# Who sends the row of maxima: ACT's own DMA queue in place of SP's, in a transformer block with cross attention and an expert FFN

## The chip, the cores and the metric

The kernel runs on one core of one Trainium2 chip. The metric is the device time of one execution in microseconds (us), lower is better; the time of before is a median of three executions. The engines are TensorE (PE), VectorE (DVE), ScalarE (ACT), GpSimd (POOL) and SyncE (SP); each runs its own list of instructions in order and waits on semaphores for the others. Before the change SP issues every plain DMA of the kernel, POOL the indirect ones, ACT none.

## The reference

For 8 batches of 512 tokens and width 256:

```
x = x + cross_attention(layernorm(x), ctx, ctx, w_proj, b_proj)   # 16 heads of 16
x = x + expert_ffn(layernorm(x), Wg, W1, W2, W3)                  # 8 experts, top 2, hidden 682
```

The attention's scores are softmax(q k / 4) over 512 keys for each of 16 heads. The kernel subtracts each query's maximum before the exponential, and that maximum is what the change is about.

## The kernel before, in words

**Attention (slots).** The first half of the execution is an order written out by hand in slots: `for slot in range(FIRST, LAST)` stands in each engine's list, and every step has a slot at which it is due, counted from its batch's first one. A batch takes 16 slots (`PER = H`); two halves of a slot do one unit each, so a batch has 32 units of scores of each of two kinds:

- `scores_ts` (line 1155): queries on the partitions. DVE takes the maximum of each row with a minus sign into `neg_max` (line 902).
- `scores_st` (line 1168), eight slots later (`AT_EXP = 8`): keys on the partitions. Here the maximum of a query runs along the free axis, so it can't be a bias. It goes in as one more row of the contraction: partition `64 * par + STACK` of `q_stack` holds the negative maximum, against a row of ones in `k_stack` (hence 49 rows, and not 48). ACT takes the exponential into `probs` (line 785), and PE weighs the values with it (line 1183).

Both kinds use the same three PSUM pairs of banks in turn. PE can fill a pair only when ACT (exponential) or DVE (maximum) has read what stood in it.

**The row of maxima.** For each batch there are four groups `g` of four heads. When DVE has the maxima of a group, PE turns them (four transposes into the miscellaneous bank, line 1197), ACT copies the 4 x 512 row to `max_row[g % 2]` in SBUF (line 802), and two DMAs of 2 KB each (`par` 0 and 1) carry it to partitions 48 and 112 of `q_stack`. `scores_st` waits for `s_mrow[g]` before the first unit of the group. The copies stand at half slots 8, 18, 26 and 34 of a batch, that is in slots 4, 9, 13 and 17; the groups' first exponentials stand in slots 8, 12, 16 and 20.

**SP's list.** SP waits for ACT's copy in slots 4, 8, 12 and 16 (`AT_MAX_ROW + 4 * g`) and then issues the two DMAs (line 567). The same list has the loads of `x_in`, `kt_in`, `v_ext`, `x_res`, the six DMAs of `k_stack` (line 549, slot 10 for the next batch) and six of `q_stack` (line 557), the stores of the FFN's split weights (line 477, after POOL's `w_lo`, slots 1, 6 and 14) with the next load of `w_in` behind them (line 468), and, in slot 17 of the last batch, `load_first_tiles` (line 503 and on), the first loads of the FFN. What stands behind a wait of SP waits too. The k parts are held by `s_kl` and by `s_b`, the scores of the batch before the current one, whose last unit is in slot 7; the copy into `k16[0]` that overwrites their source (ACT, line 864, slot 12) waits for them to land.

**ACT's list.** In each slot: exponential of half 0, miscellaneous copies of half 0 (`misc(2 * slot)`), exponential of half 1, then the copy of `heads`, the weights' upper halves (line 774), normalisations (line 790), casts, and the miscellaneous copies of half 1. All four copies of maxima stand in a half 0.

**FFN (tiles).** From about 510 us on the tokens of each expert go through two matmul layers, tile by tile; nothing of the change is in that part.

Of the kernel before, what the change touches and what calls it, by code (L numbers as in the profile page):

```python
# [18 lines left out]
STACK = 3 * D  # L19
# [74 lines left out]
AT_MAX_ROW = 4  # L94
# [45 lines left out]
def due(step, offset, of=1):  # L140

    b, left = divmod(step - offset, PER * of)
    return [b] if left == 0 and 0 <= b < B else []


def running(slot, offset):

    b, s = divmod(slot - offset, PER)
    return [(b, s)] if 0 <= b < B else []
# [8 lines left out]
def misc_use(b, name, i):  # L158
    return MISC_USE[b, name, i]


def misc_at(half_slot):
    return [MISC_AT[half_slot]] if half_slot in MISC_AT else []
# [86 lines left out]
def build(nc, xq_l, x_l, v_l, kT_l, wp_l, bias, wg_l, w12_l, w3_l, const, out):  # L250
    ctx = ExitStack()
    with ctx:
# [41 lines left out]
        max_row = [sa(f"max_row{i}", [4, T], F16) for i in range(2)]  # L294
# [62 lines left out]
        q_stack, k_stack, v_ext, probs = (q_stack0, q_stack1), (k_stack0, k_stack1), (v_ext0, v_ext1), (probs0, probs1)  # L357
# [98 lines left out]
        def _(sp):  # L456
# [76 lines left out]
            for slot in range(FIRST, LAST):  # L533
                for b in due(slot, AT_X_IN):
                    if b >= 1:
                        sp.wait_ge(s_ql, b)
                        sp.dma_start(x_in[:, :, :], xq_l[b]).then_inc(s_xin, 16)
                for b in due(slot, AT_K_IN):
                    if b >= 1:
                        sp.wait_ge(s_kl, b)  # L540
                        sp.dma_start(kt_in[:, :, :], kT_l[b]).then_inc(s_kin, 16)
                for b in due(slot, AT_K_PARTS):
                    sp.wait_ge(s_kl, b + 1)
                    if b >= 2:
                        sp.wait_ge(s_b, (b - 1) * UNITS)
                    for j, part in enumerate((0, 1, 0)):
                        for par in range(2):
                            row = 64 * par + j * D
                            sp.dma_start(k_stack[b % 2][row:row + D, :, :], k16[part][:, par, :]).then_inc(s_kd, 16)
                for b in due(slot, AT_Q_PARTS):  # L550
                    sp.wait_ge(s_mr, misc_use(b, "turn_q", 1) + 1)
                    if b >= 2:
                        sp.wait_ge(s_b, (b - 1) * UNITS)
                    for j, part in enumerate((0, 0, 1)):
                        for par in range(2):
                            row = 64 * par + j * D
                            sp.dma_start(q_stack[b % 2][row:row + D, :, :], qt16[part][:, par, :]).then_inc(s_qd, 16)
                for b in due(slot, AT_V_IN):
                    if b >= 2:
                        sp.wait_ge(s_pv, (b - 1) * 4)  # L560
                    sp.dma_start(v_ext[b % 2][:, :, :, :], v_l[b]).then_inc(s_vin, 16)
                for g in range(4):
                    for b in due(slot, AT_MAX_ROW + 4 * g):
                        sp.wait_ge(s_mr, misc_use(b, "max", g) + 1)
                        for par in range(2):
                            row = 64 * par + STACK
                            sp.dma_start(q_stack[b % 2][row:row + 1, 2 * g:2 * g + 2, :],
                                         max_row[g % 2][2 * par:2 * par + 2, :]).then_inc(s_mrow[g], 16)
                for c, off in enumerate(AT_W_OUT):
                    for e in due(slot, off):  # L570
                        keep_weights(e, c)
                for b in due(slot, AT_X_RES):
                    if b >= 1:
                        sp.wait_ge(s_mr, misc_use(b - 1, "project", 3) + 1)
                    sp.dma_start(x_res[:, :, :], x_l[b]).then_inc(s_xres_ld, 16)
                for b in due(slot, AT_X2_OUT):
                    sp.wait_ge(s_mr, misc_use(b, "project", 3) + 1)
                    hold(sp, s_held[3])
                    if b >= 1:
                        sp.wait_ge(s_x2st, b * 16)  # L580
                    sp.dma_start(out_v[b], x2[:, :, :]).then_inc(s_x2st, 16)
                if slot == 0:
                    sp.wait_ge(s_cst, 5)
                    sp.dma_start(out[TOKENS:TOKENS + SLOTS, :].rearrange("(s p) c -> p s c", p=P),
                                 fill[:, :, 0:W]).then_inc(s_pad, 16)
                    sp.dma_start(z_dram[E * REGION:E * REGION + SLOTS, :].rearrange("(s p) c -> p s c", p=P),
                                 fill[:, :, :]).then_inc(s_pad, 16)
                for h in range(2):
                    if piece_at(2 * slot + h):
                        next(early)  # L590
                for b in due(slot, AT_EARLY_LOAD):
                    if b == B - 1:
                        load_first_tiles()
# [171 lines left out]
        def _(act):  # L765
# [11 lines left out]
            def exponentials(slot, half):  # L777
                for b, s in running(slot, AT_EXP):
                    g, a, k = s // 4, s // 2, 2 * (s % 2) + half
                    u = b * UNITS + 2 * s + half  # L780
                    act.wait_ge(s_b, u + 1)
                    if s % 4 == 0 and half == 0 and b * 4 + g >= 2:
                        act.wait_ge(s_pv, b * 4 + (g - 1))
                    j = 2 * (a % 2)
                    nc.scalar.activation(probs[g % 2][:, j:j + 2, k, :], pair_banks[PLACE["exp", u] % 3], ACT.Exp,  # L785
                                         scale=0.25).then_inc(s_exp, 1)
# [6 lines left out]
            def misc(half_slot):  # L793
                for m, name, i, b in misc_at(half_slot):
# [10 lines left out]
                    if name == "turn_q":  # L805
                        ge(act, s_qd, b * 96)
                        nc.scalar.copy(qt16[i][:, :, :].rearrange("p a t -> p (a t)"), misc16).then_inc(s_mr, 1)

            def keep_turned(k, par):
                act.wait_ge(f_turn, k + 1)  # L810
                nc.scalar.copy(zt16[par][:, :, :, :].rearrange("p k a s -> p (k a s)"), turn16).then_inc(f_zt, 1)  # L811
# [31 lines left out]

            for slot in range(FIRST, LAST):
                exponentials(slot, 0)
                misc(2 * slot)
                if piece_at(2 * slot):
                    next(early)
                exponentials(slot, 1)
                for b, s in running(slot, AT_WEIGH):  # L850
                    if s % 4 == 3:
                        g = s // 4
                        q = b * 4 + g
                        act.wait_ge(s_pv, q + 1)
                        if q >= 2:
                            act.wait_ge(s_mw, misc_use((q - 2) // 4, "heads", (q - 2) % 4) + 1)
                        nc.scalar.copy(heads[q % 2][:, :], pv_bank).then_inc(s_hd, 1)  # L857
                for c, off in enumerate(AT_W_HI):
                    for e in due(slot, off):
                        high_weights(e, c)  # L860
                for b in due(slot, AT_K_HI):
                    act.wait_ge(s_kin, (b + 1) * 16)
                    ge(act, s_kd, b * 96)
                    nc.scalar.copy(k16[0][:, :, :], kt_in[:, :, :]).then_inc(s_kh, 1)
                for i in range(NT):
                    for b in due(slot, AT_X_NORM[i]):
                        act.wait_ge(s_rstd, (b + 1) * 4)
                        normalise(x_in, x_in, rstd, shift, i, s_qn)
                    for b in due(slot, AT_Z_NORM[i]):
                        act.wait_ge(s_rstd2, (b + 1) * 4)  # L870
                        ge(act, s_zl, b)
                        normalise(z_n, x2, rstd2, shift2, i, s_zn)
                for b in due(slot, AT_Q_HI):
                    act.wait_ge(s_qn, (b + 1) * NT)
                    if b >= 1:
                        act.wait_ge(s_mw, misc_use(b - 1, "turn_q", 1) + 1)
                    nc.scalar.copy(q16[0][:, :, :], x_in[:, :, :]).then_inc(s_qh, 1)
                for b in due(slot, AT_Z_HI):
                    act.wait_ge(s_zn, (b + 1) * NT)
                    ge(act, s_sc, b * 128)  # L880
                    nc.scalar.copy(z_row[:, 0, :, 0:W // 2].bitcast(F16), z_n[:, :, :]).then_inc(s_zh, 1)
                misc(2 * slot + 1)
                if piece_at(2 * slot + 1):
                    next(early)
# [481 lines left out]
```

## Time and profile before

| what | us |
|---|---|
| median of three executions | 984.34 |
| lowest and highest | 981.7, 991.81 |
| the profiled execution, own time | 979.42 |
| its span in the profile | 977.5 |
| attention, from the span's start | 0 to about 510 |
| FFN | about 510 to 977.5 |

The profiled execution is one more execution, not one of the three. Its own time is 1.9 us over its span; it lies 4.9 us below the median of the three. TensorE's mean granted clock was 0.963 of full speed.

### The profile page before, as it was taken

What the parts mean: (1) busy time and instruction counts of PE and PEld (TensorE: products, weight loads), DVE (VectorE), ACT (ScalarE), POOL (GpSimd) and SP (SyncE); (2) the same over time, 40 slices, a digit from 0 to 9 for tenths busy, and PEclk for the clock granted to TensorE, in tenths of its full rate; (3) what the DMA queues carried; (4) which work ended last, traced back from release to release, by engine and by line L of the source; (5) the groups of instructions that cost most, each with busy time, mean ns of one, the idle gap of its engine ahead of it and who ended that gap; (6) DMA issues with size and microseconds to landing.
All of it is one profiled execution on the core that took longest, in us unless ns stands there. A gap on an engine that the chain in (4) does not pass through costs nothing. (4 is left out here: it accounts for less than half of the span.)

```text
span 977.5 us, 20608 instructions
## 1 busy us (share of the span) xinstructions
PE 839.7 (86%) x6800; PEld 521.4 (53%) x6800; DVE 592.1 (61%) x1215; ACT 592.3 (61%) x951; POOL 447.6 (46%) x408
## 2 busy tenths in 40 slices
PE   0478898979789888899878987699999999999995
PEld 0112233323233322333236866599898998898995
DVE  1587887867778687797714554245445554545553
ACT  3368898987888778778683524244444444444442
POOL 4444456766858667685523644122332222233222
PEclk9998999999999999999899989799999999999998
DMA  6774746758476675555172649577543645254641
GB/s 168 191 151 157 179 153 191 146 194 169 155 195 137 219 159 180 120 145 186 60 264 83 216 131 297 161 226 225 154 130 97 178 131 138 43 163 120 198 80 22
DMA packets 66475, 154.28 MB, mean 158 GB/s; under 512 B 7280, under 2 KB 45296, under 8 KB 62576
## 3 DMA queue, kind: packets, MB, share of 16 engines
q1 hardware_dynamic: 52976, 135.63, 47.7%
q0 software_dynamic: 13440, 17.90, 9.4%
q8 instruction: 33, 0.54, 0.2%
q14 instruction: 26, 0.21, 0.1%
HBM read 129.43 MB, written 42.55 MB: 176 GB/s over the span
## 5 line engine op out<-in xcount | busy, mean ns | idle before, releaser
L902 DVE TENSOR_REDUCE neg_max<-ps 128x2 f16<-128x1024 f32 x256 | 307.7, 1220 | 80.0 <-PE ps L1155 78.6
L785 ACT ACTIVATE probs<-ps 128x1024 f32<-128x1024 f32 x256 | 257.5, 1022 | 66.1 <-PE ps L1168 64.2
L699 POOL DMA_INDIRECT out<-y,aim x72 | 112.9, 1568 | 289.1 <-DVE y L1100 240.1
L1270 PE MATMUL ps<-zt,w 128*128 128x256 f16 x792 | 217.1, 274 | 1.1 <-ACT zt L811 1.1
L1272 PE MATMUL ps<-zt,w 128*128 128x256 f16 x792 | 217.1, 274 | 0.0
L1274 PE MATMUL ps<-zt,w 128*128 128x256 f16 x792 | 217.0, 274 | 0.0
L823 ACT ACTIVATE silu<-ps 128x256 f32<-128x256 f32 x216 | 82.4, 382 | 203.2 <-PE ps L1274 196.3
L1082 DVE SCALAR_TENSOR_TENSOR hid<-ps,silu 128x256 f32<-128x256 f32 x216 | 91.7, 425 | 137.0 <-ACT silu L823 133.6
L1155 PE MATMUL ps<-k_stack,q_stack 48*128 48x512 f16 x512 | 106.9, 417 | 58.1 <-ACT probs L785 36.5
L1183 PE MATMUL ps<-probs,v_ext 128*32 128x512 f32 x1024 | 145.4, 641 | 6.1 <-ACT heads L857 5.1
L686 POOL TENSOR_TENSOR w_in<-w_in,scale_w 128x1408 f32<-128x1408 f32 (+1 forms) x24 | 62.6, 2607 | 130.6 <-ACT w_hi L774 130.5
L1168 PE MATMUL ps<-q_stack,k_stack 49*128 49x512 f16 x512 | 104.8, 407 | 10.8 <-DVE neg_max L902 9.4
L1290 PE MATMUL ps<-w,hid 128*128 128x256 f16 x360 | 100.5, 279 | 4.4 <-DVE hid L1089 4.4
L1292 PE MATMUL ps<-w,hid 128*128 128x256 f16 x360 | 100.5, 279 | 0.0
L1294 PE MATMUL ps<-w,hid 128*128 128x256 f16 x360 | 100.3, 279 | 0.0
L1270 PEld LDWEIGHTS ps<-zt,w 128*128 128x128 f16 x792 | 78.0, 98 | 12.3 <-ACT zt L811 1.3
L1168 PEld LDWEIGHTS ps<-q_stack,k_stack 49*128 49x128 f16 x512 | 25.3, 95 | 110.7 <-issue 59.4
L1100 DVE TENSOR_SCALAR y<-ps,aim 128x256 f32<-128x256 f32 x72 | 31.5, 480 | 86.4 <-PE ps L1299 86.4
L1272 PEld LDWEIGHTS ps<-zt,w 128*128 128x128 f16 x792 | 77.9, 98 | 9.7
L1274 PEld LDWEIGHTS ps<-zt,w 128*128 128x128 f16 x792 | 77.9, 98 | 9.4
L1155 PEld LDWEIGHTS ps<-k_stack,q_stack 48*128 48x128 f16 x512 | 25.4, 96 | 105.0 <-ACT probs L785 74.0
L1089 DVE TENSOR_TENSOR hid<-hid 128x256 f16<-128x256 f32 x180 | 77.7, 432 | 1.3 <-ACT hid L831 0.2
(122 smaller groups left out, 1124.4 us busy)
## 6 DMA issues: line engine op xcount, KB each, us to landing
w<-w_parts SPq DMA_DIRECT2D x36, 1408.0 KB
w<-w_parts SPq DMA_DIRECT2D x36, 768.0 KB
w_in<-in_w SPq DMA_DIRECT2D x16, 704.0 KB, 5.4
z_in<-slots SPq DMA_DIRECT2D x37, 258.0 KB, 5.3
v_ext<-in_v SPq DMA_DIRECT2D x8, 1024.0 KB, 7.7
k_stack<-k SPq DMA_DIRECT2D x48, 128.0 KB, 4.7
q_stack<-qt SPq DMA_DIRECT2D x48, 128.0 KB, 6.9
w_in<-in_w SPq DMA_DIRECT2D x8, 768.0 KB, 5.2
```

The lines of the kernel that those rows point to most:

```text
L699: nc.gpsimd.indirect_dma_start(out=out, out_offset=bass.IndirectOffsetOnAxis(ap=aim[frm][:, t, 0:1].bitcast(U32), axis=0), in_=y[frm][:, t ...
L785: nc.scalar.activation(probs[g % 2][:, j:j + 2, k, :], pair_banks[PLACE["exp", u] % 3], ACT.Exp, scale=0.25).then_inc(s_exp, 1)
L902: nc.vector.tensor_reduce(neg_max[b % 2][:, i, c:c + 3:2], pair_banks[PLACE["max", u] % 3], AX.X, ALU.max, negate=True).then_inc(s_red, 1)
L1155: mm = nc.tensor.matmul(to[:, par, :], q_stack[r][rows, a, i * P:(i + 1) * P], k_stack[r][rows, a, :], start=True, stop=True)
L1168: mm = nc.tensor.matmul(to[:, par, :], k_stack[r][rows, a, k * P:(k + 1) * P], q_stack[r][rows, a, :], start=True, stop=True)
L1183: mm = nc.tensor.matmul(pv_bank[32 * n:32 * n + 32, :], v_ext[b % 2][:, j, 4 * g + n, :], probs[g % 2][:, n, j, :], start=(j == 0), stop=( ...
L1270: nc.tensor.matmul(dst, w[:, kk, 1, cols], z16[:, kk, 0, :], start=(kk == 0), stop=False)
L1272: nc.tensor.matmul(dst, w[:, kk, 0, cols], z16[:, kk, 1, :], start=False, stop=False)
L1274: mm = nc.tensor.matmul(dst, w[:, kk, 0, cols], z16[:, kk, 0, :], start=False, stop=(kk == 1))
L1290: nc.tensor.matmul(y_bank[t], h[1], w3[par][:, 0, m, :], start=first, stop=False, skip_group_check=True)
L1292: nc.tensor.matmul(y_bank[t], h[0], w3[par][:, 1, m, :], start=False, stop=False, skip_group_check=True)
L1294: nc.tensor.matmul(y_bank[t], h[0], w3[par][:, 0, m, :], start=False, stop=False, skip_group_check=True)
```

## The change

SP's four waits a batch and its 64 DMA issues are taken out. ACT gets a function `send_rows`, called in each half slot right behind the exponential: if a copy of maxima stood in the half slot before, it waits for its own copy (`s_mr`), and issues the same two DMAs on ACT's queue. Since all copies stand in half 0, the rows are sent in half 1, behind that half's exponential and ahead of the other steps of the half.

```
@@ SP
-                for g in range(4):
-                    for b in due(slot, AT_MAX_ROW + 4 * g):
-                        sp.wait_ge(s_mr, misc_use(b, "max", g) + 1)
-                        for par in range(2):
-                            row = 64 * par + STACK
-                            sp.dma_start(q_stack[b % 2][row:row + 1, 2 * g:2 * g + 2, :],
-                                         max_row[g % 2][2 * par:2 * par + 2, :]).then_inc(s_mrow[g], 16)
@@ ACT
+            def send_rows(half_slot):
+                for m, name, g, b in misc_at(half_slot - 1):
+                    if name == "max":
+                        act.wait_ge(s_mr, m + 1)
+                        for par in range(2):
+                            row = 64 * par + STACK
+                            nc.scalar.dma_start(q_stack[b % 2][row:row + 1, 2 * g:2 * g + 2, :],
+                                                max_row[g % 2][2 * par:2 * par + 2, :]).then_inc(s_mrow[g], 16)
@@ ACT, the loop over slots
                 exponentials(slot, 0)
+                send_rows(2 * slot)
                 misc(2 * slot)
                 if piece_at(2 * slot):
                     next(early)
                 exponentials(slot, 1)
+                send_rows(2 * slot + 1)
```

## Rows read from the trace of the kernel before

**Rows 1.** The page: span, and busy time, share and instructions of each engine.

```profile
span 977.5 us, 20608 instructions
PE 839.7 (86%) x6800; PEld 521.4 (53%) x6800; DVE 592.1 (61%) x1215; ACT 592.3 (61%) x951; POOL 447.6 (46%) x408
```

**Rows 2.** Busy time by stretch: start:end, length, each engine, granted clock, DMA share, GB/s.

```profile
60.00:120.00 60.00, 48.85 (x328) 12.68 (x326) 46.13 (x53) 49.24 (x57) 26.13 (x14) 0.94 0.67 160
...
420.00:480.00 60.00, 51.36 (x359) 17.72 (x361) 50.25 (x94) 45.10 (x54) 35.95 (x38) 0.96 0.39 137
...
510.00:977.00 467.00, 433.48 (x4005) 382.55 (x4004) 221.56 (x614) 201.56 (x480) 145.54 (x125) 0.96 0.53 149
```

**Rows 3.** Waits, 60 to 480 us: who for whom, us in total, times, longest.

```profile
DVE neg_max L902 <- PE ps L1155: 63.9, 89, 2.7
...
ACT probs L785 <- PE ps L1168: 52.9, 66, 3.9
...
PE ps L1155 <- ACT probs L785: 36.2, 55, 2.2
...
ACT k L864 <- DMA k_stack<-k: 3.0, 3, 1.7
...
PE ps L1168 <- DMA q_stack<-max_row: 0.7, 1, 0.7
```

**Rows 4.** Waits of SP's queue, 60 to 480 us.

```profile
SPq L567 <- ACT max_row L802: 141.0, 24, 12.0
SPq L477 <- POOL w_lo L689: 128.4, 19, 12.8
```

**Rows 5.** The row's DMA issues: count, ns min/median/max, first and last start.

```profile
L567 SPq DMA_DIRECT2D q_stack<-max_row x64: 558/565/730, 44.2 to 490.0; - x64
```

**Rows 6.** Timeline of SP, one batch: start us, us, engine, line, out<-in, count.

```profile
221.20 0.46 SPq L468 DMA_DIRECT2D w_in<-in_w  x1
226.05 1.17 SPq L567 DMA_DIRECT2D q_stack<-max_row  x2
227.32 3.87 SPq L549 DMA_DIRECT2D k_stack<-k  x6
231.29 3.81 SPq L557 DMA_DIRECT2D q_stack<-qt  x6
...
252.47 1.18 SPq L567 DMA_DIRECT2D q_stack<-max_row  x2
```

**Rows 7.** Timeline of ACT around copies of maxima with dense work behind.

```profile
251.88 0.56 ACT L802 COPY max_row<-ps 4x512 f16<-4x512 f16 x1
252.35 1.01 ACT L785 ACTIVATE probs<-ps 128x1024 f32<-128x1024 f32 x1
253.26 0.58 ACT L790 ACTIVATE x_in<-x_in,shift,rstd 128x256 f32<-128x256 f32 x1
253.88 1.04 ACT L877 CAST q<-x_in 128x1024 f16<-128x1024 f32 x1
```

**Rows 8.** Timeline of ACT and SP around the last copy of maxima.

```profile
489.32 1.01 ACT L785 ACTIVATE probs<-ps 128x1024 f32<-128x1024 f32 x1
489.44 1.17 SPq L567 DMA_DIRECT2D q_stack<-max_row  x2
...
490.96 1.02 ACT L785 ACTIVATE probs<-ps 128x1024 f32<-128x1024 f32 x1 [0.63 <-PE ps L1168]
...
494.11 1.64 SPq L503 DMA_DIRECT2D z_in<-slots  x2
```

**Rows 9.** Timeline around the one time that PE waited for a row.

```profile
109.40 0.47 SPq L468 DMA_DIRECT2D w_in<-in_w  x1
...
110.14 1.17 SPq L567 DMA_DIRECT2D q_stack<-max_row  x2
...
116.54 0.39 PE L1168 MATMUL ps<-q_stack,k_stack 49*128 49x512 f16 x2 [0.70 <-DMA q_stack<-max_row]
```

**Rows 10.** Waits of SP's queue, 470 to 620 us.

```profile
SPq L516 <- DMA slots<-z_row,slot_u: 2.2, 1, 2.2
```

**Rows 11.** Timeline of SP: a load's issue that took longer.

```profile
125.44 1.39 SPq L468 DMA_DIRECT2D w_in<-in_w  x1
```

## The prediction, made before the changed kernel ran

> **What bounds the kernel now.** I read four views in this order. The page's first part [rows 1] gives PE 86% of the span and no other engine over 61%, but that is a mean over two halves with different limits. The table by stretches [rows 2] parts them: in the FFN, from 510 us on, PE is busy 433.5 of 467 us and ACT only 201.6; in the attention PE, DVE and ACT are all busy some 75 to 90% of each 60 us. The change touches only the attention, so at most some 450 us of the span are open to it. The waits [rows 3] say how the three engines hold each other there: DVE waits 63.9 us for PE, ACT 52.9 us for PE, and PE 36.2 us for ACT's exponentials, since all use three pairs of banks in turn. PE is busy 360.4 of the 420 us from 60 to 480 (the seven stretches of that table, the first and the last of which stand in [rows 2]; the five between them are 53.82, 51.12, 51.77, 51.10 and 52.36), so it idles 59.6 us, and 36.2 of these, 0.61, end with an exponential. With the small waits for ACT's other copies I take 0.65 as the share of an extra microsecond on ACT that comes through to the end. That is an estimate; the ends are 0.3 (ACT itself is idle about a fifth of the stretch, so a delay can be caught up) and 1.
>
> Then SP. It waits 141.0 us for ACT's copies of maxima and 128.4 us for POOL's `w_lo` [rows 4]. This looks like a prize and is not one: SP computes nothing, and its waiting costs only what somebody else then waits for. Those who wait for its transfers in the steady part are ACT before the copy into `k16`, 3.0 us in 3 times, and PE before `scores_st`, 0.7 us once [rows 3].
>
> **Removed from SP.** 64 issues of 565 ns [rows 5], 36 us of SP's time, and four waits a batch. What moves: in the batch shown, SP is done with a load at 221.66, then stands until the second group's row at 226.05, and only then issues the six k parts at 227.32 and the six q parts until 235.1 [rows 6]. The k parts' own conditions (POOL's `w_lo` of the slot, scores of slot 7) are met at about 221.7, so they start some 5.6 us earlier. ACT's 3.0 us of waiting for them disappear: 3.0 x 0.65 = 2.0 us gained. The other steps behind SP's row waits are stores of weights that wait for POOL anyway, and loads with slots to spare, costed at nothing; their cover is that no engine is recorded as waiting for them in the steady part. `load_first_tiles` gains nothing: its row's issue ended at 490.6, yet it started at 494.1 [rows 8], because it then waited 2.2 us for the scatter of tokens [rows 10], and that stays.
>
> **The row itself.** In 27 of 32 cases SP already stood waiting and issued within 0.03 us of the copy's end: the copy of [rows 7] ends at 252.44, SP issues at 252.47 [rows 6]. So the rows don't leave earlier. In ACT's queue they are no longer lined up behind SP's bulk transfers. PE waited for a row once, when it was issued 0.74 us after a 704 KB load: 0.70 us [rows 9]. Gain 0.7 us, if the own queue gets them through sooner; zero otherwise. The landing then took up to 5.2 us from the end of the issue (111.3 to 116.5); a row is wanted three slots, some 11 us, after its copy, so even beside the k and q parts, which will now be in flight at the second group's row, I expect no new wait.
>
> **Added to ACT.** 32 times: a wait for its own copy, and two issues. No ACT issue is in the trace; the nearest rows are SP's for the same transfers, 1.17 us for two [rows 6, 8]. Queued behind them on ACT are, in half 1 of the slot, the normalisations, casts, copies of `heads` and weights, and the next exponential, for which PE waits. Lower bound: SP's issues of larger transfers take 0.46 us in [rows 6], two such are 0.92 us, a little less than the exponential in front. Upper bound below. I take 1.17, as it is the same transfer.
>
> How much shows: the exponential in front is already handed to the engine, which can compute while ACT's sequencer issues. In [rows 7] the copy ends at 252.44, the exponential runs 252.35 to 253.36 and the next instruction started at 253.26. Issues from 252.47 hold the sequencer to 253.64: a delay of 0.38 us. I went through all 32 copies so: 25 have the next instruction right behind the exponential (delays of 0.31 to 0.44 us by this reckoning, 0.38 the value of the example), and 7 have a gap behind it that swallows the issue, such as the last, where the next exponential came only at 490.96 [rows 8]. Sum: 25 x 0.38 = 9.5 us of ACT.
>
> **Two queues at once.** The k and q parts, 3.87 + 3.81 us for 12 issues or 0.64 us each [rows 6], will start at about 221.7 and run to 229.5, and ACT issues the second group's row at 226.05: in the middle, in 7 of 8 batches. No row of before shows two plain queues issuing together. Bounds: nothing, or a whole issue of SP's for each of ACT's two, 1.28 us x 7 = 9.0 us. I take half, 4.5 us (an arrival at random waits half an issue), since issues of SP's do stretch at times, 1.39 us for one of 0.46 [rows 11, 6]. The Trainium skill has a rule that speaks against the change here ("Perfetto Trace Analysis", DMA Instruction — HWDGE): the block that makes descriptors is shared by the two engines that issue such DMAs, it is locked for one of them, and the lock wait is inside the issue that the profile shows. By it the term would be between 4.5 and 9.0 us and not nothing; no row here can show it. Its "DMA: Bandwidth & Descriptors" (Issuing engines are not separate DMA queues) adds that spreading DMAs over engines saves only issue time.
>
> **The sum.** ACT: 9.5 + 4.5 = 14.0 us more, 3.0 us less waiting: 11.0 x 0.65 = 7.2 us. PE's wait for a row: -0.7. Together +6.5 us, of which I take 6: 979.4 + 6 = 985.4 us for an execution like the profiled one. That one is 4.9 us below the median of the three; on the median I get 984.3 + 6 = 990.3. Since four executions of before (with the profiled one) have a middle of 983, I write 989.
>
> **Rivals.**
> - *Hidden issue.* If ACT's issues are as short as SP's short ones (0.92 us for two), the exponential hides them, and with no contention what is left is the gain: -2.0 - 0.7 = -2.7 us, 981.6 on the median. For: many issues of SP's are that short. Against: this very transfer took 558 ns at the least [rows 5].
> - *No overlap.* ACT issues only when the exponential has ended, or stalls its engine. Then each of 25 costs 1.17 + 0.09 (the overlap of neighbours in [rows 7]) = 1.26 us: 31.5 + 4.5 - 3.0 = 33.0 x 0.65 - 0.7 = +20.8 us, 1005 us. Place: the instruction behind each row's send. It decides once the delay behind a send is over 0.7 us: 25 x 0.7 + 4.5 - 3.0 = 19.0 x 0.65 is over 1%. Against: the trace's ACT instructions overlap by 0.09 us, so the sequencer runs ahead. For: ACT has not issued a DMA before, so nothing shows how the two share the sequencer.
> - *Contention and full pass-through.* The upper end of the two queues (9.0), and 0.1 us more at each send to get the emptied engine going (the cast of [rows 7], which waits for its own engine's result, starts 0.04 us behind the end, where others start 0.09 us before it, 0.13 us lost): 9.5 + 3.3 + 9.0 - 3.0 = 18.8 x 0.8 - 0.7 = +14.3, about 998 us.
> - *Faster by over 1%.* It would need some 10 us, and all recorded waits for SP's transfers in the steady part come to 3.7. It takes a wait whose recorded cause is another engine. I can't find it in the rows.
>
> **Chances.** My forecast (between +2 and +9.8 us) 0.50; hidden issue or otherwise about nothing or a small gain 0.18; contention with high pass-through 0.12; no overlap 0.13; faster by over 1% 0.07. One per cent, 9.8 us, is about what a measurement of this kernel tells from no change: its three executions span 10.1 us. So faster 0.07, same 0.68, slower 0.25. The range reaches from a gain of 6 us, 978 us, to the no-overlap case's centre less a little, 1004 us; that leaves out about 0.06 below and half of no overlap, and a little of contention, above. The forecast's own range is 985 to 994.
>
> **What would show it.** In the profile after: rows of ACT's queue with the two issues, about 0.57 us each, more where SP issues k and q parts at the same time; the instruction behind them 0.3 to 0.45 us later than the exponential's end in place of 0.09 us before it; k parts right behind the load of slot 6, 5 us earlier against the copy of maxima; no wait of ACT for `k_stack` in the steady part; PE's waits for ACT's exponentials up by some 6 us; the FFN's length unchanged. Wrong if the issues of ACT are much shorter or longer than SP's, if the exponential in front does not run beside them, if PE begins to wait for rows, or if SP, now ahead, starts bulk transfers that collide with something that I costed at nothing.

## The result and the profile after

Over 20 executions of each, the changed kernel takes 995.02 us (median; 988.22 to 1006.65), before 984.11 us (976.5 to 992.57). The ratio is 1.0117, with a 95% interval of 1.0095 to 1.0139: slower by 1.2%, some 11.5 us. The ratio and its interval leave out the runs that lie over 1.5% above the fastest of their kernel. Forecast were 989 us and about no change. The profiled execution has a span of 987.3 us, 9.8 us more than before's 977.5 [rows 1].

The page's first part, as [rows 1]; the work is the same, the span is not:

```profile
span 987.3 us, 20608 instructions
PE 842.6 (85%) x6800; PEld 521.6 (53%) x6800; DVE 593.0 (60%) x1215; ACT 595.0 (60%) x951; POOL 448.1 (45%) x408
```

The waits between engines from 60 to 480 us, as [rows 3] (line numbers have moved: 1155 is 1160, 1168 is 1173, 785 is 778, 902 is 907, 864 is 869):

```profile
DVE neg_max L907 <- PE ps L1160: 69.4, 101, 2.7
...
ACT probs L778 <- PE ps L1173: 47.6, 61, 2.1
...
PE ps L1160 <- ACT probs L778: 33.4, 55, 2.2
PE ps L1173 <- DMA q_stack<-max_row: 14.0, 7, 3.0
...
ACT probs L778 <- issue: 2.7, 8, 0.4
...
ACT o_t L797 <- issue: 2.2, 7, 0.3
ACT x_in L783 <- issue: 2.0, 6, 0.4
...
ACT k L869 <- DMA k_stack<-k: 1.0, 1, 1.0
```

Three things are to be seen. PE's waits for ACT's exponentials did not go up, as forecast, but down, from 36.2 to 33.4 us. PE's wait for the row of maxima went from 0.7 us, once, to 14.0 us in 7 times: once in each of the first seven batches, at the second group. And ACT has a new kind of idle time, "issue", in pieces of 0.3 to 0.4 us: the exponential, the `o_t` copy and the `x_in` row hold 6.9 us of it.

The waits of SP's queue in the same stretch, as [rows 4]: the 141.0 us for ACT's copies are gone, and the wait for POOL's `w_lo` is 174.9 us longer.

```profile
SPq L477 <- POOL w_lo L682: 303.3, 22, 22.7
SPq L541 <- POOL k L718: 9.9, 5, 4.1
```

The timeline of the same batch, one engine after the other, as [rows 6]; ACTq is ACT's own queue:

```profile
222.77 0.46 SPq L468 DMA_DIRECT2D w_in<-in_w  x1
223.33 4.09 SPq L549 DMA_DIRECT2D k_stack<-k  x6
227.52 5.13 SPq L557 DMA_DIRECT2D q_stack<-qt  x6
```

```profile
225.69 0.57 ACT L795 COPY max_row<-ps 4x512 f16<-4x512 f16 x1 [0.28 <-PE ps L1202]
226.17 1.01 ACT L778 ACTIVATE probs<-ps 128x1024 f32<-128x1024 f32 x1
226.29 1.21 ACTq L809 DMA_DIRECT2D q_stack<-max_row  x2
227.55 1.02 ACT L778 ACTIVATE probs<-ps 128x1024 f32<-128x1024 f32 x1 [0.37 <-issue]
...
233.79 0.39 PE L1173 MATMUL ps<-q_stack,k_stack 49*128 49x512 f16 x2 [1.80 <-DMA q_stack<-max_row]
```

The k parts now start at 223.33, 2.93 us before the copy ends at 226.26; in [rows 6] they started at 227.32, behind the row. The row leaves ACT between 226.29 and 227.50, beside them, and PE gets it only at 233.79, 6.3 us later. PE had been ready at 231.99. Over the seven batches the k parts start 0.1 to 4.3 us before the copy ends, and PE gets the row 5.9 to 7.5 us after its issues. The k parts themselves land later too: the median from issue to landing is 6.8 us, before 4.7.

How long ACT's issues took, as [rows 5]:

```profile
L809 ACTq DMA_DIRECT2D q_stack<-max_row x64: 565/566/1201, 44.1 to 496.1; - x64
```

The attention ends 6.1 us later in this pair of profiles: the last `scores_st` starts at 509.7 us, before at 503.6. The rest of the 9.8 us comes in the first tiles of the FFN, at the two loads of tokens that PE waits for before and after (PE starts behind them at 621.68 and 641.50, before at 614.70 and 631.67). PE's two waits there are 16.3 us together, before 13.9. I made no run on that part.

### The profile page after: what moved, and what is told of

It is laid out like the page before. It is cut to its first block and busy times, and to the rows that moved or that the text cites. A ratio compares the mean times of both kernels' runs of the same rounds, so it can differ in the third digit from the quotient of the medians.

```text
span 987.3 us, 20608 instructions
## 1 busy us (share of the span) xinstructions
PE 842.6 (85%) x6800; PEld 521.6 (53%) x6800; DVE 593.0 (60%) x1215; ACT 595.0 (60%) x951; POOL 448.1 (45%) x408
```

## The experiments

All edits are against the changed kernel or the kernel before, as said; each ratio is to the kernel before on the same chip, with its 95% interval. Two theories stand against each other. *Collision*: SP, freed of its wait for the second group's copy, sends the k and q parts ahead of and beside that group's row, and the row lands too late. *Stall*: the issues hold ACT's sequencer, and what shows behind the exponential is the loss.

**SP keeps its waits, ACT sends.** Changed kernel, with the waits back in SP's list and no row to send behind them:

```
+                for g in range(4):
+                    for b in due(slot, AT_MAX_ROW + 4 * g):
+                        sp.wait_ge(s_mr, misc_use(b, "max", g) + 1)
```

> ACT sends all rows as in the changed kernel, but SP keeps its four waits a batch for the copies of maxima, so that its k and q parts start when they did before. Collision theory (the loss is PE's wait for the second group's row, which now travels beside the 12 k and q parts): if what matters is that the parts start no earlier, PE's waits for rows fall from 14.0 to under 3 us and the ratio to before to about 1.003; if a row on a queue of its own loses to the parts even when both start together, PE still waits 5 to 14 us and the ratio stays near 1.01. Stall theory (the loss is ACT's sequencer, 25 delays of some 0.35 us): PE's waits for rows may go, yet the ratio stays at about 1.010.

Ratio 1.0023 [0.9998, 1.0049]. Its waits from 60 to 480 us have no wait of a PE matmul for a row, and ACT's idle time from issues is what it was in the changed kernel:

```profile
ACT probs L781 <- issue: 3.0, 8, 0.4
...
ACT x_in L786 <- issue: 2.0, 6, 0.4
ACT o_t L800 <- issue: 2.0, 6, 0.4
```

So with all 32 sends on ACT the kernel is 0 to 5 us slower than before, and giving SP nothing but its old waits takes away most of the loss. It was mostly the timing of SP's other transfers that mattered, not who sends the row.

**Second group's row on SP, the others on ACT.** ACT's `send_rows` for g in (0, 2, 3), SP's old code for g = 1.

> The second group's row stays on SP, ahead of the k and q parts as before; ACT sends the other three (24 of 32 sends). Collision theory: PE's waits for rows are under 1 us, the ratio is 1.000 to 1.004. Stall theory: three quarters of the delays are left, the ratio is about 1.009.

Ratio 1.0066 [1.0041, 1.0092], between the two. PE doesn't wait for rows, as the collision theory has it, but the ratio is above its 1.004 and below the stall theory's 1.009. It was run again, below.

**Only the second group's row on ACT.** The reverse: ACT sends 8 of 32 rows, SP the rest, so SP no longer waits for the second group's copy.

> Only the second group's row is sent by ACT (8 of 32 sends), the others by SP as before. Collision theory: PE waits for this row about 14 us in 7 times as in the changed kernel, the ratio is 1.008 to 1.012. Stall theory: a quarter of the delays, the ratio is about 1.003.

Ratio 1.0118 [1.0070, 1.0166], the whole loss with a quarter of the sends. Its waits from 60 to 480 us:

```profile
PE ps L1180 <- DMA q_stack<-max_row: 17.4, 7, 3.6
```

Here the stall theory, as the cause of most of the loss, fell.

**All rows on SP, the second group's behind the parts.** Kernel before, one number:

```
-                    for b in due(slot, AT_MAX_ROW + 4 * g):
+                    for b in due(slot, 10 if g == 1 else AT_MAX_ROW + 4 * g):
```

> ACT sends nothing. SP sends all rows, but the second group's only after the k and q parts of slot 10, so that the parts start early and the row stands behind them in the one queue. Collision theory: the row leaves about 3 us later than from ACT and then lines up behind 1.5 MB, PE waits 14 to 35 us for it, the ratio is 1.01 to 1.03. Stall theory: no delay of ACT, the ratio is 1.000.

Ratio 1.0515 [1.0475, 1.0555]: the direction was right, the size far over what was expected. No ACT issue at all, and the suspected cost enlarged:

```profile
PE ps L1168 <- DMA q_stack<-max_row: 47.4, 7, 9.9
```

47.4 us of PE waiting cost some 50 us of time, about one for one.

**Waits kept, and ACT's two issues parted.** As the first, but `send_rows` issues `par` 0 one half slot behind the copy and `par` 1 two half slots behind it, so each stands behind its own exponential:

```
+                for par in range(2):
+                    for m, name, g, b in misc_at(half_slot - 1 - par):
+                        if name == "max":
```

> As the run with SP's waits kept, but ACT issues one DMA of 0.57 us behind each of two exponentials in place of two behind one. If the 0.35 us delays behind the sends are what is left of the loss (1.0023), they vanish from ACT's idle time (8.1 us recorded as issue, to under 1) and the ratio is 0.998 to 1.001. If ACT's delays are absorbed anyway, the ratio stays at 1.002.

Ratio 0.9990 [0.9962, 1.0018]. Around a copy with dense work behind it, to be set beside [rows 7]:

```profile
193.99 0.56 ACT L798 COPY max_row<-ps 4x512 f16<-4x512 f16 x1
194.45 1.01 ACT L781 ACTIVATE probs<-ps 128x1024 f32<-128x1024 f32 x1
194.57 0.57 ACTq L812 DMA_DIRECT2D q_stack<-max_row  x1
195.37 0.58 ACT L786 ACTIVATE x_in<-x_in,shift,rstd 128x256 f32<-128x256 f32 x1
195.98 1.05 ACT L885 CAST q<-x_in 128x1024 f16<-128x1024 f32 x1
196.10 0.57 ACTq L812 DMA_DIRECT2D q_stack<-max_row  x1
```

The instruction behind the exponential starts 0.92 us after it, as in before (0.91): one issue of 0.57 us fits under an exponential of 1.01 us, two don't. No wait of ACT for an issue is left in the stretch; PE waits 1.9 us, in 2 times, for rows. Against the first run this is 0.0033, but with an interval of about 0.004 either way it is not clear of nothing. It is the best of the versions with ACT as sender, and the same as before within its interval.

**Only the wait for the second group's copy kept.** As the first, with `for g in (1,)`.

> ACT sends all rows; SP keeps only the wait for the second group's copy, the one ahead of the k and q parts. If this single wait is what was lost, the ratio is that of the run with all four waits, 1.002, within 0.003. If SP's freedom elsewhere costs too (the run with the second group's row on SP had 1.0066 without any wait for rows, and its PE clock rose some 20 us later at the start), it is about 1.006.

Ratio 1.0024 [1.0000, 1.0048]. One wait of SP's four does what the four did, within the intervals.

**Parts held until the row has landed.** Changed kernel, and ahead of the k parts:

```
+                    if b >= 1:
+                        sp.wait_ge(s_mrow[1], b * 32)
```

> The changed kernel with the k parts held until both DMAs of the second group's row have landed: the row travels with no parts beside it. Collision theory: no wait of PE for rows; the parts start 2 to 4 us after the copy and land later, so that ACT waits up to 3 us a batch before its copy into k16. Ratio 1.003 to 1.010, made of ACT's waits and not PE's. Stall theory: the changed kernel's 1.012.

Ratio 1.0104 [1.0060, 1.0147]: just over the range that was expected. PE doesn't wait for rows; ACT waits instead, for the late k parts ahead of its copy into `k16` (from 60 to 480 us):

```profile
ACT k L871 <- DMA k_stack<-k: 9.7, 6, 3.3
```

So early parts and late parts both cost here, by different waits. This run also measures how fast a row lands with no parts beside it, since SP's next issue is what it lets go. The timeline of ACT's and SP's queues:

```profile
175.31 1.19 ACTq L811 DMA_DIRECT2D q_stack<-max_row  x2
177.59 1.87 SPq L551 DMA_DIRECT2D k_stack<-k  x3
236.78 1.17 ACTq L811 DMA_DIRECT2D q_stack<-max_row  x2
239.03 1.20 SPq L551 DMA_DIRECT2D k_stack<-k  x2
```

From the end of the row's issues (176.50, 237.95) to SP's first k part it takes 1.1 us, as in five of the seven batches, against 5.9 to 7.5 us in the changed kernel. In the other two a load of SP's left shortly ahead of the row: 2.3 us, and 3.4 us in the second batch, where 768 KB started 0.75 us before it.

**Only the q parts held.** Changed kernel; SP waits for the second group's copy between the k and the q parts.

> The changed kernel with only the six q parts held behind the second group's copy; the six k parts leave early as in the changed kernel, ahead of the row. If it is the transfers in front of the row that hold it, most of the wait stays (8 to 14 us of PE in 7 times, ratio 1.008 to 1.012). If it is what comes in beside and behind it, most goes (under 5 us, ratio 1.002 to 1.005).

Ratio 1.0084 [1.0053, 1.0114]; PE waits as long as ever:

```profile
PE ps L1175 <- DMA q_stack<-max_row: 16.9, 7, 3.4
```

But the edit held almost nothing. In the changed kernel the q parts start only when the k parts' six issues are done, 0.05 to 0.10 us behind them; here they start 0.10 to 0.32 us behind them:

```profile
224.27 4.07 SPq L549 DMA_DIRECT2D k_stack<-k  x6
228.64 4.77 SPq L559 DMA_DIRECT2D q_stack<-qt  x6
228.65 1.31 ACTq L811 DMA_DIRECT2D q_stack<-max_row  x2
236.26 0.39 PE L1175 MATMUL ps<-q_stack,k_stack 49*128 49x512 f16 x2 [1.93 <-DMA q_stack<-max_row]
```

So this run doesn't part the k parts from what comes behind the row. It is nearly a repeat of the changed kernel, and shows that two nearly equal kernels can come out 0.0033 apart, 1.0084 and 1.0117, which is within their intervals. The second batch, with a load of 768 KB 0.7 us ahead of the row in all four cases, tells more of the order. From the end of the row's issues to landing it took 3.4 us with no parts in flight (the run before), 5.2 with the k parts right behind the row ([rows 9]), at most 5.2 with both started together (the first run), and 5.9 with the k parts 0.17 us ahead of it (the changed kernel). By these four, one profile each, what comes right behind the row slows it too, and what goes ahead slows it a little more, past the slack.

**The same order, with the row in SP's queue.** Kernel before; SP issues the k parts, waits for the copy, issues the row, then the q parts.

> ACT sends nothing. SP issues the six k parts early, then waits for the second group's copy and issues its row, then the six q parts: the timing of the run with the q parts held, with the row in SP's queue and not in ACT's. If a queue of its own brings the row past transfers that were issued earlier, PE waits longer here than the 16.9 us of that run, 20 us or more, and the ratio is 1.012 or more. If the queue makes no difference, PE waits 14 to 19 us, and the ratio is 1.005 to 1.010 (no delays of ACT).

PE waits 16.7 us in 7 times, in total the same as the 16.9 with the row in ACT's queue:

```profile
PE ps L1175 <- DMA q_stack<-max_row: 16.7, 7, 5.5
```

The equal totals are chance, though. In the first two batches the copy was ready while SP was still issuing k parts, so the row left 2.4 and 4.3 us behind the copy, and PE waited 4.6 and 5.5 us (with ACT as sender 2.5 and 1.9). In the other five the row left at most 1.2 us behind the copy, and PE waited 6.6 us together, against 12.5. One batch of each kind:

```profile
109.71 4.39 SPq L549 DMA_DIRECT2D k_stack<-k  x6
114.15 1.29 SPq L555 DMA_DIRECT2D q_stack<-max_row  x2
121.01 0.61 PE L1175 MATMUL ps<-q_stack,k_stack 49*128 49x512 f16 x2 [5.46 <-DMA q_stack<-max_row]
...
233.16 1.30 SPq L555 DMA_DIRECT2D q_stack<-max_row  x2
234.56 4.34 SPq L564 DMA_DIRECT2D q_stack<-qt  x6
239.61 0.39 PE L1175 MATMUL ps<-q_stack,k_stack 49*128 49x512 f16 x2 [0.67 <-DMA q_stack<-max_row]
```

From the end of its issues the row took 4.9 to 6.3 us here, ahead of the q parts, and 6.1 to 7.8 us in ACT's queue with the q parts starting beside it. So the k parts ahead of the row are enough for a wait, and ACT's queue did not bring the row past them; it took about 1 us longer there, and whether the q parts beside it or the queue make that, the runs don't part. The ratio is 1.0151 [1.0114, 1.0187], above the expected 1.010, and what is in it beside the row's wait stays open. TensorE's mean granted clock over the timed runs was 0.949 here and 0.955 in the run with the q parts held, so part of it may come with the clock; that is not shown.

**Second group's row on SP, again.**

> The kernel with the second group's row on SP and the others on ACT once more, on another chip. Its 1.0066 stood above the 1.0023 and 1.0024 of two kernels with more sends on ACT. If that was scatter (its profile had a late rise of PE's clock), it comes out at 1.000 to 1.004 now; if it is the kernel, at 1.005 to 1.008.

Ratio 1.0065 [1.0030, 1.0100]: not scatter. Part of it shows in the pace of PE in the first batch. The `scores_ts` matmuls take 610 to 620 ns at first and 384 later. In both profiles of this kernel the step comes at some 85 to 91 us, in the changed kernel's at about 70. The granted clock reads 1.00 in all of these stretches, so it is the length of the matmuls that shows the step. In the kernel before, from 72 to 78 us, they take 614 to 623 ns at a granted clock of 0.50: the slow pace is that of the lower level, 1.2 GHz. Here is the kernel's second profile from 70 to 80 us, then the changed kernel's (count, busy us, mean ns):

```profile
L1167 PE MATMUL ps<-k_stack,q_stack 48*128 48x512 f16 x8 | 2.5, 611 | 1.7 <-ACT probs L785 1.7
```

```profile
L1160 PE MATMUL ps<-k_stack,q_stack 48*128 48x512 f16 x14 | 2.7, 383 | 2.6 <-ACT probs L778 2.6
```

But the profile of the run that keeps only the second group's wait has the late step too, at 1.0024. Why this kernel is slower than that one is open.

**The changed kernel with ACT's two issues parted.** SP without waits, `send_rows` as in the fifth run.

> The changed kernel with ACT's two issues parted, one behind each of two exponentials; SP free of waits as in the changed kernel. The collision stays and the second DMA of the row leaves up to 1.5 us later: PE's waits for rows 14 to 22 us. ACT's delays go. Collision theory: the ratio stays at 1.009 to 1.014. Stall theory: 1.000 to 1.004.

Ratio 1.0080 [1.0051, 1.0110]; PE waits 15.1 us for rows, ACT none for issues. Less than the 1.009 expected, and 0.0037 less than the changed kernel, as between the first and the fifth run (0.0033). But the run that nearly repeats the changed kernel has 1.0084, about the same.

## Why the prediction was wrong

What the runs give, in parts of the time before: the collision, 0.0094 (1.0117 - 1.0023) or 0.0090 (1.0080 - 0.9990), each give or take 0.003 to 0.004; with the near repeat in the changed kernel's place, 0.0061. ACT's delays, 0.0033 and 0.0037 (the two pairs with and without parted issues), each with about as much uncertainty, and 0.0004 with the near repeat. So more than half of the 1.0117 is the collision, 6 to 9 us, and ACT's delays are somewhere from nothing to some 4 us. That the two terms add up to about the whole is no test, since all four are differences of the same four ratios; what speaks for them is that each comes out alike both ways. The kernel with the second group's row on SP, 0.0042 slower than the one with SP's waits kept and with fewer sends on ACT, fits neither term and is open. The forecast had ACT's term and not the collision.

- **The step that failed** is the one on the row itself: "even beside the k and q parts, which will now be in flight at the second group's row, I expect no new wait", priced at -0.7 us. It came to 6 to 9 us more, with 14.0 us of PE's waiting. Both of its numbers were off. The slack was put at "three slots, some 11 us", from a mean slot; at the second group it is 5.7 us (copy's end 226.26, PE ready 231.99). [Rows 9] held the same: the row's issues from 110.14, PE ready at 115.84. And the landing was taken from that same case, 5.2 us behind one load (of 768 KB, not 704: ACT's next `w_hi` has 1536 columns), as an upper bound; behind six k parts it is 5.9 to 7.5 us, alone 1.1 us. Read together there, the slack from the start of the row's issues is 5.7 us, and 1.2 us of issues with 5.2 of landing are 6.4. That is 0.7 us too much, the wait recorded there, and no room at all.
- **"SP's waiting costs only what somebody else then waits for"** was right about the gain and blind to the other side: the wait for ACT's copy was also what kept the row ahead of the 1.5 MB of parts. That they would start earlier was foreseen (5.6 us; it was 4.0 us against [rows 6] by the clock, and 4.2 against the copy's end) and booked only as a gain. That gain came: ACT's waits for them fell from 3.0 to 1.0 us. Whether the loss is all in PE's waits is not shown. In the three kernels with all sends on ACT and one or more of SP's waits kept, TensorE's mean granted clock over the timed runs was 0.959 to 0.960, as in the kernel before beside them; in the changed kernel it was 0.9545, and in the other five in which PE waits over 10 us for rows 0.935 to 0.955. The runs don't tell whether the lower clock is part of the cost or goes with it.
- **ACT's issue** was right as a mechanism: 566 ns against 565, beside the exponential. The next instruction starts some 1.35 us behind the exponential's start and not 0.91, a delay of 0.43 us where 0.38 was worked out, in 25 of 32 places, as many as forecast: 10.8 us in place of 9.5. The pass-through looks too high: the pairs put the cost at 3.3 to 3.6 us, a third of it and not 0.65, but their uncertainty reaches from nothing to about 0.65.
- **Two queues at once** was booked at 4.5 us. The two issues beside SP's k and q parts took 1.17 to 1.28 us in the seven batches, against 1.17: 0.2 us in all. The Trainium skill's rule of a shared and locked block ("Perfetto Trace Analysis", DMA Instruction — HWDGE) would have made it 4.5 to 9.0. The lock, if it is there, cost ACT next to nothing; the measurement decides.
- **"In ACT's queue they are no longer lined up behind SP's bulk transfers"** did not hold: in its own queue the row took 5.9 to 7.5 us behind k parts in SP's, and 1.1 us with none in flight. The Trainium skill's "DMA: Bandwidth & Descriptors" (Issuing engines are not separate DMA queues) says that DMAs run on the same 16 DMA engines, whichever engine started them, and the trace agrees.
- **The rivals.** No overlap fell with ACT's delays of 0.43 us, far under its 0.7; hidden issue and contention of the issues fell too. The time came out near the third's, some 0.3% under it, but by chance and not by its mechanism. The unchanged length of the FFN was off too, by 3.7 us in this profile.

## What to carry to other kernels

Before a wait is taken from a DMA queue, list what is queued behind it and what it keeps in front: a wait can be the only thing that lets a small urgent transfer go ahead of a large one. The slack of such a transfer is to be read at the place itself, from the copy's end to the consumer's start, and not worked out from a mean step. Here a second issuing engine didn't bring a small transfer past bulk that was already under way. And if an engine must issue DMAs, one issue behind each long instruction can stay hidden where two do not.

## What the runs showed of the hardware

A row, in two transfers of 2 KB, landed 1.1 us after its issues with nothing else near, and 5.9 to 7.5 us after them with six transfers of 128 KB started 0.2 to 4.3 us before, in another queue. ACT's sequencer issues a DMA of 0.57 us while its engine computes an exponential handed over before it, and an issue costs the same there as on SP. PE's matmuls of 512 columns went from some 611 to 383 ns within the first batch, at about 70 us in the changed kernel and 85 to 91 us with the second group's row on SP, while the granted clock read 1.00 throughout. The longer time is that of a stretch whose granted clock read 0.50, so the record of 1.00 doesn't seem to hold there; the runs don't tell what sets the moment.
